# Attention sums and outputs fetched through DRAM in a feature-major layout, instead of being turned back and forth on TensorE

## What is computed

```python
qkv = x @ Wqkv                                     # x: 32 x 512 x 256
logits = einsum('bihd,bjhd->bhij', q, k) / 4 + SLOPES * (j - i), causal
out = einsum('bhij,bjhd->bihd', softmax(logits), v).reshape(B, T, 256)
x = layernorm(x + out @ Wout)
h = silu(x @ wg.T) * (x @ wu.T)
x = layernorm(x + h @ wd.T)
```

## Time and profile before

| what | value |
|---|---|
| median of 3 runs | 2136.32 us (2136.15 to 2137.07) |
| the profiled execution's own time | 2136.29 us |
| its span | 2134.6 us |
| TensorE matmul, busy | 1983.0 us (93%) |
| VectorE, busy | 1595.1 us (75%) |
| ScalarE, busy | 1223.5 us (57%) |
| GpSimd, busy | 928.5 us (43%) |
| chain that ended last | PE 80%, DVE 10%, ACT 5%, DMA 2% |
| mean granted TensorE clock | 0.981 |
| DMA | 229.09 MB, 48.5% of 16 engines' span |

### The profile page before, as it was taken

The page is one execution under the profiler, slowest core; times in us unless marked ns, Lnnn a source line. Parts: engine busy times, 40 slices in busy tenths (PEclk is TensorE's granted clock), DMA queues, the critical chain, the costliest instruction groups (busy, mean ns, idle before and its releaser), DMA issues.

```text
span 2134.6 us, 47883 instructions
## 1 busy us (share of the span) xinstructions
PE 1983.0 (93%) x19236; PEld 1550.0 (73%) x19236; DVE 1595.1 (75%) x2765; ACT 1223.5 (57%) x1999; POOL 928.5 (43%) x1924
## 2 busy tenths in 40 slices
PE   4779999999999999999999999999999999999986
PEld 3557777777777777777777777777877877777766
DVE  4557777787777787777778777778777778777754
ACT  1446656555655656655655665565565665566552
POOL 0123444444444453444454444444344445444444
PEclk8789999999999999999999999999999999999998
...
GB/s 205 103 120 105 101 112 118 96 112 114 115 112 110 103 108 106 128 103 108 113 100 112 121 109 111 116 97 114 106 122 109 106 109 102 111 125 91 100 16 21
DMA packets 148830, 229.09 MB, mean 107 GB/s; under 512 B 13552, under 2 KB 64496, under 8 KB 148592
## 3 DMA queue, kind: packets, MB, share of 16 engines
q1 hardware_dynamic: 148608, 226.02, 48.5%
...
## 4 chain that ended last, share of the span: by engine, by line
PE 80%; DVE 10%; ACT 5%; DMA 2%; issue 1%; SPq 1%; POOL 0%; POOLq 0%; DVEq 0%
PE pair L495 72%; PE pair L498 8%; DVE row_max L801 7%; ACT probs L726 3%; DVE staged_lo L786 2%; ACT staged_hi L704 2%; DMA q_rows<-max_lo 1%; SPq L471 0%; DMA q_rows<-bounce 0%; DMA probs<-L_attn_Wout 0%; SPq L480 0%; DMA bounce<-staged_lo 0%; DVE row_max L803 0%; DVE xt_lo L786 0%; DVE x1t_lo L786 0%
## 5 line engine op out<-in xcount | busy, mean ns | idle before, releaser
L726 ACT ACTIVATE probs<-pair 128x1024 f32<-128x1024 f32 x640 | 627.1, 1027 | 150.1 <-PE pair L495 149.8
L903 POOL TENSOR_SCALAR_AFFINE_SELECT probs<-probs 128x256 f32<-128x256 f32 (+1 forms) x896 | 371.5, 440 | 445.9 <-ACT probs L726 445.1
L910 POOL TENSOR_TENSOR h_lo<-h_full,h_hi 128x256 fp32r<-128x256 f32 x384 | 283.2, 738 | 507.6 <-ACT h_hi L751 496.9
L803 DVE TENSOR_REDUCE row_max<-pair 128x8 f32<-128x1024 f32 x256 | 312.6, 1221 | 115.2 <-PE pair L495 114.7
L801 DVE TENSOR_REDUCE row_max<-pair 128x2 f32<-128x1024 f32 x256 | 311.9, 1218 | 71.2 <-PE pair L495 71.2
L495 PE MATMUL pair<-q_rows,k_rows 64*128 64x512 f32 (+3 forms) x2048 | 321.0, 370 | 38.4 <-DMA q_rows<-max_lo 20.8
L495 PE MATMUL pair<-k_rows,q_rows 52*128 52x512 f32 (+3 forms) x2048 | 299.6, 351 | 60.2 <-DVE staged_lo L786 26.1
L495 PE MATMUL pair<-probs,v_ones 128*32 128x512 f32 (+3 forms) x4096 | 319.3, 441 | 0.8 <-ACT probs L726 0.8
L495 PEld LDWEIGHTS pair<-q_rows,k_rows 64*128 64x128 f32 x2048 | 167.8, 188 | 157.2 <-ACT probs L726 92.2
L495 PEld LDWEIGHTS pair<-k_rows,q_rows 52*128 52x128 f32 x2048 | 179.0, 190 | 122.9 <-DVE row_max L801 62.9
L704 ACT ACTIVATE staged_hi<-pair 128x512 fp32r<-128x512 f32 x128 | 76.6, 599 | 269.9 <-PE pair L495 260.5
...
## 6 DMA issues: line engine op xcount, KB each, us to landing
bounce<-staged_hi SPq DMA_DIRECT2D x128, 256.0 KB
bounce<-staged_lo SPq DMA_DIRECT2D x128, 256.0 KB
q_rows<-bounce SPq DMA_DIRECT2D x128, 256.0 KB, 5.2
k_rows<-bounce SPq DMA_DIRECT2D x128, 256.0 KB, 6.2
x_sb<-L_attn_x SPq DMA_DIRECT2D x32, 512.0 KB, 10.4
k_rows<-bounce SPq DMA_DIRECT2D x128, 128.0 KB, 5.5
q_rows<-bounce SPq DMA_DIRECT2D x128, 128.0 KB, 6.7
...
```

The lines of the kernel that those rows point to most:

```text
L726: scalar.activation(probs[g][:, tile, :, :], pair[:, :, :], ACT.Exp, scale=scale).then_inc(s_exp, 1)
L803: vector.tensor_reduce(maxima[:, QB2_PARTS:QB0 + 1, :, p].rearrange("p b s -> p s b"), pair[:, :, :].rearrange("p s (b n) -> p s b n", n=P ...
L903: made = pool.affine_select(out=diagonal, in_=diagonal, compare_op=ALU.is_ge, fill=0.0, base=0, pattern=[[0, diagonal.shape[1]], [1, P]], ...
L910: pool.tensor_tensor(h_lo[:, m, :], h_full[(n_split_h[step] - 1) % H_BUFFERS][:, :], h_hi[:, m, :].bitcast(F32), ALU.subtract).then_inc(s_ ...
```

## The change

The unit's attention output is no longer turned to tokens-on-partitions and back. After each `pv_copy` SyncE sends `pv_t` (256 KB) to DRAM (`send`). After both groups of a unit it fetches (`fetch`) the sums, one row of each head, laid out over 128 partitions by 32 columns (`sums`), and the outputs of all 8 heads, features on the partitions (`attn`, now 128 by 512 per unit). VectorE takes one reciprocal of the sums per unit (`recip`), SyncE sends it to DRAM (`send_recip`, 16 KB) and fetches it repeated for the 16 features of each head (`fetch_recip`, 256 KB). In the next rest GpSimd multiplies (`divide`), ScalarE copies the high part (`attn_hi`) and GpSimd subtracts (`attn_lo`). The steps `turn` and `transposed("attn")` are gone. The output projection of a batch moves from the odd rest to the even rest after it; each half FFN moves one rest later; `values` move to the end of the odd rest before, the x transposes stay in the even rest, x1's go to the odd. `norm1` of the first half is added behind the last `gate_up` and ahead of `down`. The plan has one step w more. Cut from the diff: the tallies, the declarations of buffers and semaphores, the removed entries of `split_tiles` and `bank_emptied`, and the removed waits of the `attn` transposes.

```diff
@@ -88,7 +88,7 @@
         self.order, self.norms_due = [], []
         self.banks, self.before = {}, {}
         self.user, self.used = [None] * BANKS, list(range(-BANKS, 0))
-        for w in range(-2, self.units + 4):
+        for w in range(-2, self.units + 5):
             self.attention(w)
             self.rest(w)
 
...
@@ -147,6 +147,9 @@
                 else:
                     self.resume(("pv", u, g, 1), ("pv", u, g, 0))
                     self.add("pv_copy", u, g)
+                    self.add("send", u, g)
+                    if g == 1:
+                        self.add("fetch", u)
                     held = None
         self.norms()
         if self.has(w):
...
@@ -167,15 +170,9 @@
             if side == 1:
                 self.add("spread", u)
 
-    def values(self, b):
-        for t0 in (0, 2):
-            self.take("values", b, t0)
-            self.add("values_out", b, t0)
-
-    def turn(self, u, g):
-        if self.has(u):
-            self.take("turn", u, g)
-            self.add("divide", u, g)
+    def values(self, b, t0):
+        self.take("values", b, t0)
+        self.add("values_out", b, t0)
 
     def max_row(self, u):
         if self.has(u):
...
@@ -201,58 +198,59 @@
         self.add("norm2", b, part)
 
     def rest(self, w):
-        k = w // 2
-        ffn, part = k - 2, w % 2
+        k, part = w // 2, 1 - w % 2
+        ffn = k - 2 - part
         has_ffn = 0 <= ffn < self.batches
+        has_out = part == 1 and 0 <= k - 2 < self.batches
         if self.has(w + 1):
             self.add("gather", w + 1)
+        if self.has(w - 3):
+            self.add("divide", w - 3)
         if part == 0:
-            if 0 <= k < self.batches:
-                self.values(k)
             if has_ffn:
                 self.transposed("x1", ffn)
-            self.turn(w - 2, 1)
-            self.turn(w - 1, 0)
-            if 0 <= k - 1 < self.batches:
-                self.add("load_residual", k - 1)
-            if 0 <= k + 1 < self.batches:
-                self.transposed("x", k + 1)
-                if k + 2 < self.batches:
-                    self.add("load_x", k + 2)
-            if has_ffn:
-                self.gate_up(ffn, 0, range(0, 2))
-            self.max_row(w)
-            if has_ffn:
-                self.gate_up(ffn, 0, range(2, 6))
             self.project(w + 2, 0)
-            if has_ffn:
-                self.down(ffn, 0)
-            self.project(w + 2, 1)
-        else:
-            done = k - 1
-            has_done = 0 <= done < self.batches
-            self.turn(w - 2, 1)
-            self.project(w + 2, 0)
-            self.turn(w - 1, 0)
             if w == -1:
                 self.ffn_weights()
-            if has_done:
-                self.transposed("attn", done)
-            if has_ffn:
-                self.gate_up(ffn, 1, range(0, 3))
             self.max_row(w)
-            if has_done:
-                self.project_out(done, 0)
-            if has_ffn:
-                self.gate_up(ffn, 1, range(3, 6))
-            if has_done:
-                self.project_out(done, 2)
-            if has_ffn:
-                self.down(ffn, 1)
-            if has_done:
-                self.add("norm1", done, 0)
-                self.norms_due.append(("norm1", done, 2))
-            self.project(w + 2, 1)
+        if has_ffn:
+            self.gate_up(ffn, part, range(0, 2))
+        if self.has(w - 3):
+            self.add("attn_hi", w - 3)
+            self.add("attn_lo", w - 3)
+        if part == 1:
+            self.max_row(w)
+        if self.has(w - 2):
+            self.add("recip", w - 2)
+            self.add("send_recip", w - 2)
+        if part == 0 and 0 <= k - 1 < self.batches:
+            self.add("load_residual", k - 1)
+        if has_ffn:
+            self.gate_up(ffn, part, range(2, 3))
+        if part == 1 and 0 <= k + 1 < self.batches:
+            self.transposed("x", k + 1)
+            if k + 2 < self.batches:
+                self.add("load_x", k + 2)
+        if has_ffn:
+            self.gate_up(ffn, part, range(3, 4))
+        if has_out:
+            self.project_out(k - 2, 0)
+            self.project_out(k - 2, 2)
+        if has_ffn:
+            self.gate_up(ffn, part, range(4, 6))
+        if has_out:
+            self.add("norm1", k - 2, 0)
+            self.norms_due.append(("norm1", k - 2, 2))
+        if part == 1:
+            self.project(w + 2, 0)
+        if has_ffn:
+            self.down(ffn, part)
+        self.project(w + 2, 1)
+        if part == 0 and 0 <= k + 1 < self.batches:
+            self.values(k + 1, 0)
+            self.values(k + 1, 2)
+        if self.has(w - 2):
+            self.add("fetch_recip", w - 2)
 
     def ffn_weights(self):
         self.add("as_float")
...
@@ -346,6 +347,8 @@
         result = [sb(f"result{i}", [P, 2, dim]) for i in range(2)]
 
         bounce = nc.dram_tensor("bounce", [2, 4, HEAD_DIM, UNIT_PAIRS, 2, tokens], F32, kind="Internal").ap()
+        pv_bounce = nc.dram_tensor("pv_bounce", [2, 2, GROUP, 2, HEAD_DIM, tokens], F32, kind="Internal").ap()
+        recip_bounce = nc.dram_tensor("recip_bounce", [2, UNIT_HEADS, tokens], F32, kind="Internal").ap()
         edge_copy = nc.dram_tensor("edge_copy", list(edge_rows.shape), F32, kind="Internal").ap()
 
         pairs = [ps(f"pair{i}", [P, 2, BANK]) for i in range(BANKS // 2)]
...
@@ -479,6 +484,40 @@
                             row = s * HALF + MAX_ROW + r
                             sync.dma_start(q_rows[u % 2][row:row + 1, :, :].bitcast(F32),
                                            source[s * UNIT_PAIRS:(s + 1) * UNIT_PAIRS, :].bitcast(F32)).then_inc(s_max_stored[u % 2], 16)
+                elif kind == "send":
+                    u, g = key
+                    z = u % 2
+                    e.wait_ge(s_pv_copy, n_pv_copy["pv_copy", u, g])
+                    if u >= 2:
+                        e.wait_ge(s_fetched[z], (u // 2) * 16 * 2)
+                    sync.dma_start(pv_bounce[z, g].rearrange("h c d t -> (h c d) t"), pv_t[g][:, :]).then_inc(s_sent[z][g], 16)
+                elif kind == "fetch":
+                    u, = key
+                    z = u % 2
+                    for g in range(2):
+                        e.wait_ge(s_sent[z][g], (u // 2 + 1) * 16)
+                    if u >= 2:
+                        e.wait_ge(s_attn_lo, n_attn_lo["attn_lo", u - 2])
+                        e.wait_ge(s_recip, n_recip["recip", u - 2])
+                    parts = pv_bounce[z].rearrange("g h c d t -> (g h) c d t")
+                    sync.dma_start(sums[z][:, :], parts[:, 1, 0, :].rearrange("h (a n) -> h a n", n=sums[z].shape[1])).then_inc(s_fetched[z], 16)
+                    sync.dma_start(attn[z][:, :], parts[:, 0, :, :]).then_inc(s_fetched[z], 16)
+                elif kind == "send_recip":
+                    u, = key
+                    z = u % 2
+                    e.wait_ge(s_recip, n_recip["recip", u])
+                    if u >= 2:
+                        e.wait_ge(s_recip_fetched[z], (u // 2) * 16)
+                    sync.dma_start(recip_bounce[z].rearrange("h (a n) -> h a n", n=sums[z].shape[1]), small_recips[z][:, :]).then_inc(s_recip_sent[z], 16)
+                elif kind == "fetch_recip":
+                    u, = key
+                    z = u % 2
+                    e.wait_ge(s_recip_sent[z], (u // 2 + 1) * 16)
+                    if u >= 2:
+                        e.wait_ge(s_divide, n_divide["divide", u - 2])
+                    r = recip_bounce[z]
+                    wide = bass.AP(tensor=r.tensor, offset=r.offset, ap=[list(r.ap[0]), [0, HEAD_DIM], list(r.ap[1])])
+                    sync.dma_start(recips[z][:, :], wide).then_inc(s_recip_fetched[z], 16)
                 elif kind == "norm2":
                     b, part = key
                     e.wait_ge(s_norm2, 2 * n_norm2[step])
...
@@ -628,18 +664,10 @@
                                       weights, j == 0, j == blocks - 1, tile_position=(0, 32 * h))
                     made.then_inc(s_pv, 1)
 
-                elif kind == "turn":
-                    u, g = key
-                    bank = bank_of(step)
-                    e.wait_ge(s_pv_copy, n_pv_copy["pv_copy", u, g])
-                    for t in range(blocks):
-                        made = turn(bank[:, t * P:(t + 1) * P], pv_t[g][:, t * P:(t + 1) * P])
-                    made.then_inc(s_work, 1)
-
                 elif kind == "out":
                     b, t0 = key
                     bank = bank_of(step)
-                    e.wait_ge(s_lo, n_lo["split_lo", "attn", b, 1])
+                    e.wait_ge(s_attn_lo, n_attn_lo["attn_lo", 2 * b + 1])
                     terms = [(w, a, c) for w, a in ((wout_hi, attn_hi), (wout_lo, attn_hi), (wout_hi, attn_lo)) for c in range(kd)]
                     for t in range(2):
                         for n, (w, a, c) in enumerate(terms):
...
@@ -730,8 +756,15 @@
```

(47 more changed lines are left out.)

32 lines of the change are left out of this document (16 added, 16 removed).

## The result

The changed kernel takes 2364.59 us (median of 4 runs, 2350.54 to 2366.08), the kernel before 2136.24 beside it: ratio 1.106 [1.101, 1.110]. The profiled execution has a span of 2364.4 us and a mean granted clock of 0.923 (before 0.981). The forecast was 2185, in a range of 2120 to 2245: right in direction, 180 us short.

A forecast was written before the change was run, and what follows sets the result against it. TensorE, busy 93% of the span, was taken as the bound. Steady batches of 64.2 against 63.2 us gave about +30, head -7 and tail +26 on 2136.3: 2185 us, range 2120 to 2245.

The forecast's parts named there:

- the wait behind `norm1`: Even rest: GpSimd's last `h_lo` stands behind `norm1`, 17.1 against 14.3 on TensorE, a 2.8 us wait; rest 19.1 us.
- odd rest and the stage behind it: Odd rest 16.6 us, including waits of 0.4 and 0.5; the attention stage behind it 0.5 us shorter, 14.0.
- Head: Start of the run: rest 4 loses 8.5 us of TensorE work and gains 2.86; taken as -7 (-9 to 0).
- tail: End of the run: half an FFN without attention beside it, late `norm1` and the last unit's chain, together +26 (15 to 32).
- the chain forecast at +8: Tail: the last unit's `norm2` store, `fetch_recip`, divide, hi and lo hold the last output projection and `h_lo`, +8 us.
- I cost all DMAs at nothing: SyncE and DMAs: the new transfers add 0 us; the `recip` fetch lands at 14 to 20, wanted at 19.9.
- The cover named: SyncE's queue: `gather` at most about 1.5 us late, its data wanted a whole rest later.
- The waits for gather and store are absent in the steady part: Steady part before the change: no waits for gather and store, held against late DMA round trips costing 2 us a batch.
- rival C: DMA round trips too late: `recip` holds VectorE's queue or `gather` comes late, 2 us a batch, 2245 us; chance 0.13.
- rival D: TensorE's clock falls after each wait of 3 us, +4 us a batch, 2305 us; chance 0.04.
- for a wait of 3 us there is no row: TensorE's clock: 1.00 with waits up to 0.45 us, lower after 9.54 us; no profile evidence at 3 us.
- B: Even rest: VectorE not held up by `max_hi`, wait 1.3, rest 17.5, batch 62.1 us, total 2123 us; chance 0.15.

The follow-up runs named there:

- the clock kept: The changed kernel with 22 filler transposes before the last part of `down` in even rests and 30 before the first scores of odd units: 2302.87 us, ratio 1.078.

## Why the prediction was right and wrong

**Right: the wait behind `norm1`, the term it decided on.** GpSimd's and TensorE's timelines of the kernel after, in the even rest that starts at 1007.26:

```profile
1019.96 0.74 POOL L932 TENSOR_TENSOR h_lo<-h_full,h_hi 128x256 fp32r<-128x256 f32 x1 [1.78 <-ACT h_hi L784]
1020.80 0.19 POOL L952 TENSOR_SCALAR var<-moments 128x2 f32<-128x2 f32 x1
...
1022.15 1.09 POOL L958 TENSOR_SCALAR x<-x,mean,rstd 128x256 f32<-128x256 f32 x2
1023.20 0.72 POOL L932 TENSOR_TENSOR h_lo<-h_full,h_hi 128x256 fp32r<-128x256 f32 x1
```

```profile
1023.98 0.79 PE L534 MATMUL pair<-wdown_t,h_hi 128*128 128x256 f32 x2 [2.48 <-POOL h_lo L932]
...
1025.00 1.05 PE L534 MATMUL pair<-xt_hi,wqkv_hi 128*128 128x512 f32 x2
```

The last `h_lo` stands behind a whole `norm1` of 2.4 us; TensorE waits 2.48 (forecast 2.8) and goes on 16.7 us into the rest (17.1). With the clock kept, this rest takes 18.77 (19.1). VectorE stood 0.95 us before `max_lo` (1.2), and GpSimd's two new operations take 1.28 and 1.29 us each (1.35). Repairing the order brought 3.8 us a batch, of which 1.1 were given back behind it.

**Right: odd rest and the stage behind it.** Where VectorE does not wait for the fetch the odd rest takes 16.7 to 16.9 (16.6) and the attention stage behind it 14.0 (14.0): the half microsecond from `staged_lo` of the earlier trace rows did fall away. Head -4.7 (-7) and tail +31 (+26) were near. In the tail TensorE waits 8.57 us for the last `attn_lo`, the chain forecast at +8.

**Wrong: "I cost all DMAs at nothing", +92 us.** The step asked whether each new transfer lands in time for its own reader. That held nearly everywhere: VectorE waits for the fetch 13.2 us in the whole run, in 16 of 64 units, and only four of the 17 odd rests in the table are longer for it. The step did not ask what the transfer does to those behind it. `fetch` puts 256 KB in front of `gather` and `store_max`, the second `send` 256 KB more, which no run took away, and the moved residual load puts 512 KB behind them in the same rest; the share there goes from 0.59 to 0.96, and the row maxima, wanted 16.7 us after the rest's start, come 3.11 us too late, 3.11 x 29.5 = 92. The cover named was `gather`'s ("its data are wanted a whole rest later"); `store_max`, in the same sentence's queue, is wanted in the next stage. "The waits for gather and store are absent in the steady part", the argument against rival C, held for a share of 0.59 and said nothing of one near 1. C had the kind right, a DMA that lands too late, and its price of 2 us a batch was near the 3.11. It had the place wrong: it looked at `recip` and `gather`, and `store_max` was the one.

**Wrong: rival D at 0.04, another +82 us.** Windows of the kernel after behind the 3.39 us wait at 1062.23:

```profile
1062.50:1064.50 2.00, 2.00 (x17) 1.45 (x16) 0.88 (x1) 1.31 (x2) 0.34 (x1) 0.50 0.52 192
...
1066.50:1068.50 2.00, 2.00 (x14) 0.67 (x8) 0.84 (x1) 0.04 (x1) 0.41 (x1) 0.54 0.53 204
1068.50:1070.50 2.00, 1.71 (x30) 1.11 (x32) 1.48 (x2) 1.29 (x2) 0.77 (x2) 1.00 0.27 102
```

0.50 is the level of 1.2 GHz, 1.00 that of 2.4 GHz: the first matmuls behind the wait run at half clock, the later ones at full. The means above give (20.15 - 18.77) + (15.44 - 14.01) = 2.8 us a batch, 82 us. The step that failed is "for a wait of 3 us there is no row": the forecast's own wait of 2.8 us lay between rows of 0.45 and 9.54 us, and it took the side of 0.45, so the term stands at nothing in the sum. The rule of the Trainium skill (TensorE: Matmul & The Clock Gate, HAM oscillation), which the prediction weighed as the case to fear, has the clock fall once in each period of a loop behind a wait; this trace agrees, in all of 19 even rests behind 2.48 us. D's own price of 4 us was for one long stretch; two short ones cost 2.8.

**The forecast with its DMA term right.** The run with the short fetch is close to the kernel that the forecast had in mind: the wait behind `norm1` is there, the wait for the maxima is not. It takes 2211 us, 26 over the 2185. Its even rest is 0.87 us above the 18.77 with the clock kept, 0.87 x 29.5 = 26: the clock behind the forecast's own wait, and only in 11 of 19 batches.

**The sum with both terms mended:** 2185 + 92 + 82 = 2359. What is left to 2364 is smaller and of both signs: odd rests above 16.6 (+13, 7 of them in the four that waited for the fetch), the even rest's work below the forecast (-10), head and tail (+7), and a rest of -5 that means over the middle of the run leave.

**The range** treated C and D as two unlikely and separate cases. They go together: a late landing makes a wait that lowers the clock at the scores (+42 of the 82 us), and the forecast wait lowers it in the even rest, in 11 of 19 batches without the late landing and in all of 19 with it. A forecast that itself holds a wait of nearly 3 us in every batch should have given D much more weight. B's stages add up to 62.3 us a batch and not to 62.1, so its time would be 2129 for 2123; that would move the lower end of the range a little and nothing else.
